# Order of pieces, row turns and weight splits in the expert loop, and when the attention weights are loaded

## The reference

```python
x = x + 0.5 * ffn(layernorm(x))
x = x + attention(layernorm(x))        # 16 query heads, 8 key heads of 32, rotary, tanh soft cap, causal
x = x + 0.5 * ffn(layernorm(x))

# ffn(inp): x = w_norm * inp * rsqrt(mean(inp^2) + eps)
# router: softmax over 32 experts, the best 4 of each token
# each expert takes at most 128 tokens: y = (silu(xg @ w_gate) * (xg @ w_up)) @ w_down   (256 -> 176 -> 256)
# shared part, for all tokens: sigmoid(x @ w_shared_gate) * ((silu(x @ sw_gate) * (x @ sw_up)) @ sw_down)   (256 -> 704 -> 256)
# out = inp + experts' outputs, weighted and added to their tokens' rows + shared part
```

## Time and profile before

| | us |
|---|---|
| median of 3 runs | 946.34 (943.54 to 947.62) |
| the profiled execution | 943.53 |
| its span, first to last instruction | 941.8 |
| TensorE busy | 899.0 (95%) |
| VectorE busy | 731.3 (78%) |
| ScalarE busy | 579.3 (62%) |
| GpSimd busy | 513.9 (55%) |
| share of TensorE in the chain that ended last | 52%, VectorE 21%, issue 13%, GpSimd 6% |
| granted TensorE clock, mean | 0.997 |

### The profile page before, as it was taken

How to read it: one execution, slowest core, us unless ns; L and a number is a source line. 1 busy time by engine, 2 the same in 40 slices (tenths; PEclk the granted TensorE clock), 3 DMA queues, 4 the chain that set the end, 5 groups by cost and what they waited for, 6 DMA issues and landing times.

```text
span 941.8 us, 18520 instructions
## 1 busy us (share of the span) xinstructions
PE 899.0 (95%) x6246; PEld 688.6 (73%) x6246; DVE 731.3 (78%) x1768; ACT 579.3 (62%) x922; POOL 513.9 (55%) x537
## 2 busy tenths in 40 slices
PE   8999998999999999999999999989999989999997
PEld 6778886877878856666666666558788868778786
DVE  6998786765565889999998999988887867665545
ACT  6676744344444478878887888867667433444432
POOL 6343304456653588887887788934333045566530
PEclk9999999999999999999999999999999999999999
DMA  8143245777874610010001002004432457778735
GB/s 259 50 139 103 75 132 149 176 174 183 192 166 101 201 46 24 23 43 24 23 23 45 22 11 82 21 12 129 142 98 74 127 155 175 174 178 199 162 39 177
DMA packets 95515, 101.93 MB, mean 108 GB/s; under 512 B 18768, under 2 KB 86736, under 8 KB 95440
## 3 DMA queue, kind: packets, MB, share of 16 engines
q1 hardware_dynamic: 83152, 83.17, 29.3%
q0 software_dynamic: 12288, 17.83, 11.1%
HBM read 65.44 MB, written 35.54 MB: 107 GB/s over the span
## 4 chain that ended last, share of the span: by engine, by line
PE 52%; DVE 21%; issue 13%; POOL 6%; ACT 5%; DMA 2%; DVEq 0%; POOLq 0%; ACTq 0%
PE gu L91 6%; PE gu L93 6%; PE gu L92 6%; PE zT L1058 4%; PE pj_at L91 3%; PE pv_at L1815 3%; PE pj_at L93 3%; PE pj_at L92 3%; PE down L91 2%; PE down L93 2%; PE down L92 2%; PE scores_at L1799 2%; POOL out L841 2%; DVE turned_at L2057 2%; POOL rows L833 2%
## 5 line engine op out<-in xcount | busy, mean ns | idle before, releaser
L1144 ACT CAST a_hi<-act_gu 128x512 fp32r<-128x512 f32 x96 | 59.3, 618 | 94.6 <-DVE act_gu L1396 68.2
L91 PE MATMUL gu<-x_hi,gu_hi 128*128 128x512 f32 x264 | 113.4, 429 | 1.3 <-DVE act_gu L1396 1.2
L833 POOL DMA_INDIRECT rows<-z_rows,slots x64 | 71.1, 1110 | 67.5 <-DVE slots L1383 48.5
L1917 ACT ACTIVATE capped_at<-scores_at 128x2048 f32<-128x2048 f32 x64 | 93.1, 1454 | 20.6 <-PE scores_at L1799 20.4
L93 PE MATMUL gu<-x_lo,gu_hi 128*128 128x512 f32 x264 | 103.9, 393 | 0.0
L92 PE MATMUL gu<-x_hi,gu_lo 128*128 128x512 f32 x264 | 103.3, 391 | 0.0
L1925 ACT ACTIVATE probs_at<-capped_at 128x2048 f32<-128x2048 f32 x64 | 95.2, 1487 | 2.5
L1994 POOL TENSOR_SCALAR_AFFINE_SELECT probs_at<-probs_at 128x1024 f32<-128x1024 f32 x64 | 85.6, 1342 | 9.6 <-ACT probs_at L1925 8.8
L91 PE MATMUL down<-down_hi,a_hi 128*128 128x256 f32 x300 | 89.8, 299 | 0.6 <-DVE a_lo L1406 0.4
L1058 PE MATMUL zT<-w_gu,xT 128*128 128x352 f32 x256 | 88.4, 468 | 0.1
L841 POOL DMA_INDIRECT acc<-base,slots x32 | 51.2, 1599 | 65.2 <-DMA acc<-base,slots 53.3
(11 more groups left out here) (269 smaller groups left out, 2807.4 us busy)
## 6 DMA issues: line engine op xcount, KB each, us to landing
w_gu<-in_w_gate SPq DMA_DIRECT2D x64, 176.0 KB
w_gu<-in_w_up SPq DMA_DIRECT2D x64, 176.0 KB
w_down<-in_w_down SPq DMA_DIRECT2D x64, 176.0 KB
z_rows<-z SPq DMA_DIRECT2D x16, 512.0 KB, 3.6
acc<-base SPq DMA_DIRECT2D x10, 512.0 KB, 3.4
out<-base SPq DMA_DIRECT2D x10, 512.0 KB, 3.2
xn_at<-acc SPq DMA_DIRECT2D x16, 256.0 KB, 2.8
x<-xn_at SPq DMA_DIRECT2D x16, 256.0 KB, 2.1
```

Of the source, the lines that this page charges most:

```text
L91: nc.tensor.matmul(out, w_hi, x_hi, start=first, stop=False)
L833: pool.indirect_dma_start(out=gathered_rows[:, n, :], out_offset=None, in_=m.z_rows, in_offset=bass.IndirectOffsetOnAxis(ap=slots[:, e:e + ...
L1144: nc.scalar.copy(a_hi[rows_, mt, :], act_gu[rows_, mt % 2, :]).then_inc(a_hi_ready, 1)
L1917: nc.scalar.activation(capped[:, u % 2, :, 0:n], scores[:, :, 0:n], ACT.Tanh, scale=QK_SCALE / SOFTCAP).then_inc(capped_ready, 1)
```

## The change

TensorE, in every period: before, `gate_up_expert(e)`, `turn_rows(e+1)`, first piece, `down_expert(e-1)`, `turn_products(e)`, then the second (and third) piece. Changed: `gate_up_expert(e)`, first piece, `turn_rows(e+1)`, second piece, `down_expert(e-1)`, `turn_products(e)`, third piece if there is one. The lists of ScalarE and VectorE follow: the follow-up of the second piece comes earlier, and the split of the down weights (`high_down`, `low_down`) goes from behind the split of the products to between the follow-ups of the first two pieces.

SyncE: Wq, Wk and Wv are loaded after the first routing slot, behind a wait for the splits of the shared gate and up weights; Wo is loaded in four groups of four DMAs as experts 28 to 31 finish their gate/up matmuls.

```diff
+    def gate_up_split(self, engine):
+        engine.wait_ge(self.lo_made, self.gu_total)
...
-    def load_projections(self, sp):
+    def load_projections(self, sp, shared_weights):
+        shared_weights.gate_up_split(sp)
         for dst, name in ((self.q, "Wq"), (self.k, "Wk"), (self.v, "Wv")):
             sp.dma_start(dst[:], self.ins[name].rearrange("(k p) n -> p k n", p=P)).then_inc(self.loaded, 16)
+
+    def load_output(self, sp, n):
         wo = self.ins["Wo"].rearrange("(g j r d) n -> g r j d n", g=2, r=REP, d=HD)
-        for group in range(2):
-            for r in range(REP):
-                for j in range(4):
-                    sp.dma_start(self.m.o[j * HD:(j + 1) * HD, REP * group + r, :], wo[group, r, j]
-                                 ).then_inc(self.loaded, 16)
+        group, r = divmod(n, REP)
+        for j in range(4):
+            sp.dma_start(self.m.o[j * HD:(j + 1) * HD, n, :], wo[group, r, j]).then_inc(self.loaded, 16)
...
                 slot(b, *ROUTES[b])
+                if b == 0 and attention_weights:
+                    attention_weights.load_projections(sp, weights)
...
             if attention_weights:
-                attention_weights.load_projections(sp)
+                for n in range(4):
+                    reached(sp, gu_done, E - 3 + n)
+                    attention_weights.load_output(sp, n)
...
 # on_tensor
                 gate_up_expert(e)
+                first_piece, second_piece, *third_piece = pieces_beside(e)
+                piece(first_piece)
                 if e + 1 < E:
                     turn_rows(e + 1)
-                first_piece, *later_pieces = pieces_beside(e)
-                piece(first_piece)
+                piece(second_piece)
                 if e > 1:
                     down_expert(e - 1)
                 turn_products(e)
-                for p in later_pieces:
+                for p in third_piece:
                     piece(p)
...
 # on_scalar
                 silu_expert(e)
-                first_piece, *later_pieces = pieces_beside(e)
+                first_piece, second_piece, *third_piece = pieces_beside(e)
                 followup(first_piece)
+                high_down(e)
+                followup(second_piece)
                 if e > 1:
                     scale(e - 1)
                 high_products(e)
-                high_down(e)
-                for p in later_pieces:
+                for p in third_piece:
                     followup(p)
...
 # on_vector
-                first_piece, *later_pieces = pieces_beside(e)
+                first_piece, second_piece, *third_piece = pieces_beside(e)
                 followup(first_piece)
+                low_down(e)
+                followup(second_piece)
                 low_products(e)
                 if lists:
                     list_tokens(2 + e // 2)
-                low_down(e)
-                for p in later_pieces:
+                for p in third_piece:
                     followup(p)
```

## The result

The changed kernel takes 955.27 us (median of 4 runs, 953.71 to 961.5), the kernel before 944.94 us in the same comparison: ratio 1.0121, 95% interval 1.0065 to 1.0177. The whole interval lies above 1, so it is slower. (A ratio is worked out from all the runs and is not the quotient of the two medians, which is 1.0109 here.) The forecast was 948.9 us with no clear change as the likeliest; the time lies inside the range, but it is a clear change for the worse, and it is near the rival of the falling clock (954.0).

A forecast was written before the change was run, and what follows sets the result against it. TensorE, busy 95% of the span, was taken as the bound. Terms of +3.6 us (expert parts) and -1.0 us (behind the first) gave +2.6 on 946.3, so 948.9 us; range 936 to 956.

The forecast's parts named there:

- +3.6 us in the expert parts: Both expert parts: new waits behind the in-order engines outweigh the cover gained, +1.8 us in each part.
- nothing for the clock: The sum held no term for falls of TensorE's granted clock behind new waits; they appeared only in a rival.
- -1.0 us behind the first part: End of first expert part: removing the load burst lets adds finish earlier, so TensorE's 1.04 us wait goes.
- the signs listed for a right prediction: L1067 under 4 us; L1049 waits; first down projection and L950 wait about 2 us; burst and 309.84 wait gone.
- the wait at 309.84: TensorE's 1.04 us wait behind the first part, caused by the late last add; forecast to disappear.
- rival (2): Clock halves for 3.4 us behind three more waits at experts 0, 3, 30, losing 1.7 us each: 954.0; chance 0.18.
- The walk of experts 0 to 3: Start of each expert part: late splits delay expert 4's start by 2.1 us, expert 0's 1.1 among it.
- Experts 4 to 31: Rest of each expert part: late periods cost +2.25 us, vanished waits return 2.2, so about 0.
- the last add at 300.7: First part's last scatter-add: forecast to start at about 300.7 where it was 301.09, with TensorE 1.8 us later.
- The burst's gap of 6.8 us: Adds near 282 to 288 us, held apart by attention-weight loads; removing the burst returns 2.5 us to the adds.
- Loads: Routing part: SyncE's extra wait and three 0.4 us issues, hidden before later loads are read; taken as 0.

The follow-up runs named there:

- the filling: Changed kernel plus unread dummy transposes on TensorE ahead of the long waits at experts 0, 3 and 30, both expert parts: 952.69 us, 1.0093.
- The filled kernels: Kernel before with new loads, new order in one part alone, its three long waits filled with dummy transposes: second part 947.02 us, 1.0006; first 949.56 us, 1.0032.
- the splits last: Changed kernel with the split of the down weights put back behind the products' split on ScalarE and VectorE: 950.07 us, 1.0038.
- the order alone: Changed kernel with the attention weights loaded where the kernel before loads them, only the order of expert periods new: 959.06 us, 1.0166.
- the last version: Changed kernel with old order throughout the first part and for experts 0 to 3 and 30 of the second, new loads kept: 942.76 us, 0.9962.
- the one late add: Kernel before with GpSimd's second scatter-add held until the third expert's output is scaled: 944.35 us, 1.0002.

## Why the prediction was right or wrong

In short: the sum had +3.6 us in the expert parts, nothing for the clock and -1.0 us behind the first part. The traces have +8.6 us in the expert parts, 7.2 of them from clock falls, and +2.0 us behind the first. Of the signs listed for a right prediction all came but one: the wait at 309.84 was to go and it grew. The sign of rival (2), half clock in more than one place, came too.

**The walk of experts 0 to 3: right.** First down projection forecast at 153.4, measured 153.39. Expert 4 was forecast 2.1 us later. Its first gate/up matmul starts at 172.53, where the earlier trace rows has 168.37, with expert 0 at 146.86 in both: +4.16. Of that, half of the fall at 154.7 is 1.7 and half of the 0.8 us that lie behind 171.8 is 0.4, which leaves +2.05. In the second part it is 792.60 - 765.76 = 26.84 against 781.32 - 759.80 = 21.52: +5.32, less 1.7 and 1.55 (3.1 us behind 789.6) = +2.05. The waits themselves came at 0.82 (forecast 0.9), 1.85 (2.1) and 2.27 (2.55).

**Experts 4 to 31: mis-sized.** Forecast 0. From expert 4 to the last `silu_e` the changed kernel takes 295.06 - 172.53 = 122.53, less 1.3 for the rest of the fall: 121.2; before 291.12 - 168.37 = 122.75. That is -1.5. By the same working the second part has 121.2 against 122.5: -1.3. Which of the small waits that I added up for experts 9 to 24 came shorter was not taken apart. Without the falls the order thus costs +0.5 and +0.8, not +1.8, in each part.

**The clock: the term at zero that decided.** This is the step that failed: the sum had new waits of over 2 us at experts 0, 3 and 30 and no fall of the clock behind any of them. The falls cost 3.4 us in the first part and 5.0 - 1.2 = 3.8 in the second (its own against before's). With the rest: 2.05 - 1.5 + 3.4 = +3.95 (measured 3.93) and 2.05 - 1.3 + 3.8 = +4.55 (4.65); these sums are bookkeeping on one trace each and close by the way they are made, so the test is the filling. Rival (2) had this mechanism, its places and its size per fall (1.7 us); it asked for three falls more and there were five. I gave it 0.18, since the wait of 1.51 us at expert 30 had kept its clock in one part and lost it in the other. The new waits are longer (1.85 to 2.62 us) and lost it in five of six places. The filled kernels show the clock's cost apart from the waits' for the second part: 1.0050 to 1.0006. For the first they don't show it in time, only in length of the part in one trace of two.

**-1.0 us at the end of the first part: wrong sign.** I put the last add at 300.7; it starts at 305.65. (The terms that I gave, 301.09 - 2.5 + 0.8 + 1.8, make 301.2.) The burst's gap of 6.8 us did go, but the last add is late for other reasons: the add of expert 3 is 6.1 us late and not the 2.6 that I allowed (0.8 and 1.8), and what carries a delay on to the last add is open, as said above. TensorE's wait grew from 1.04 to 1.88 us:

```profile
314.60 0.50 PE L91 MATMUL gu<-x_hi_third,gu_hi 128*128 128x512 f32 x1 [1.88 <-DVE act_gu L1406]
```

and half clock followed (from 315.1). Nor was there a whole microsecond to win. With the splits last this wait is 0.28 us, no fall lies between the parts, and from the last `silu_e` of the first part to the first of the second it takes 470.07 us, where the kernel before, with its 1.04 us, takes 470.14.

The start of the second part is the later of two ends. One is TensorE's: in the six traces in which it waits 1.2 us or less for the attention rows, those 470 us are 470.07 to 470.28. The other is the adds': in the other eleven the start follows the last add. Take 761.26 plus the delay of the last add against the earlier trace rows plus half of what part of the fall lies behind the wait: for the changed kernel 761.26 + 4.56 + 1.7 = 767.5 (767.22 measured). The same sum gives for the order alone (last add at 309.34) 772.0 (771.48), the filled one 768.0 (768.72), old order in experts 0 to 3 and 30 764.2 (764.06), the new order in the first part alone 771.4 (771.36), and the last version 766.4 (766.45). It is off by at most 1.0 us in all eleven, so it tells the bound and not tenths. By this reading 4.6 of the 6.0 us by which the second part starts late are the adds' and the rest the clock's; how TensorE's falls inside the first part share in the adds' delay is not shown. The kernel with the loads alone is the plain case of the other end: its last add is so early (299.35) that TensorE was the bound.

**Loads: right at zero.** Expert 0 starts at 146.86 in both kernels, so the routing part in front of it lost nothing to the loads put there.

**Open.** What sets the distance of two adds, and with it the share of the loss in the first part: with the same first part (old order, new loads) the last add started between 299.35 and 303.67, and behind the one late add the next four came 4.1 to 4.3 us apart, where those of before took 4.8 to 5.5 in the same place. Nor is it settled which falls of the clock repeat in every execution.

## What to carry to other kernels

Before giving one wait a longer cover, walk the in-order engines behind it: what is now ahead of their next step becomes a wait elsewhere, and a wait of 2 us can cost nearly twice its length (1.7 us of work per fall), because the clock may fall behind it. The waits of 1.2 to 1.6 us did this less often (8 of 31, against 22 of 29), and no fall stood behind a shorter wait alone. Price each new wait of some 2 us with the fall included. Ask of each part of a kernel which chain ends it: here the first expert part ends with a chain of adds and TensorE nearly together, and only the second with TensorE alone, so the shorter first part (140.25 us) was lost again at once in its trace, and the version that shortens only the second (140.56) came out faster. Overlapping intervals leave open that the two versions differ.

## What the hardware showed unexpectedly

Waits of 1.85 to 2.62 us behind dense matmuls were followed by half clock in five of six places, for 3.4 us each time, in which the engine was busy throughout; in other executions the half clock began inside such a wait and lasted 6.8 us (new order in the second part alone, from 766.7). More matmuls made the part shorter: 82 useless transposes took 2.96 us off the second expert part. And a chain of scatter-adds in DRAM, one landing before the next, ran at 3.9 to 4.3 us an add at its best and at 4.4 to 4.7 on average over the last 28, whichever order TensorE had; what sets that pace is open.
